# The first layer norm of a graph network: its normalising steps on GpSimd instead of VectorE

## What is computed

```python
def layer_norm(x, w, b):
    mu = jnp.mean(x, axis=-1, keepdims=True)
    var = jnp.var(x, axis=-1, keepdims=True)
    return (x - mu) * jax.lax.rsqrt(var + EPS) * w + b

h = gatv2(x, src, dst, W1s, b1s, W1d, b1d, attn1).reshape(N, DIM)
h = layer_norm(h + x, ln1_w, ln1_b)
out = gatv2(h, src, dst, Wos, bos, Wod, bod, attno).reshape(N, DIM)
```

## Time and profile before

| | before |
|---|---|
| median of three runs | 1425.2 us |
| lowest, highest | 1421.56, 1425.47 us |
| profiled execution | 1419.24 us |
| its span | 1417.4 us |
| VectorE busy | 943.6 us, 67% |
| GpSimd busy | 611.8 us, 43% |
| ScalarE busy | 564.3 us, 40% |
| TensorE busy | 1029.6 us, 73% |
| mean granted TensorE clock | 0.854 |

### The profile page before, as it was taken

The page is one execution under the profiler, slowest core; times in us unless marked ns, Lnnn a source line. Parts: engine busy times, 40 slices in busy tenths (PEclk is TensorE's granted clock), DMA queues, the critical chain, the costliest instruction groups (busy, mean ns, idle before and its releaser), DMA issues.

```text
span 1417.4 us, 15860 instructions
## 1 busy us (share of the span) xinstructions
PE 1029.6 (73%) x5499; PEld 859.4 (61%) x5499; DVE 943.6 (67%) x1678; ACT 564.3 (40%) x735; POOL 611.8 (43%) x581
## 2 busy tenths in 40 slices
PE   5956455556551677798999999618267998999982
PEld 5954333333330676797778787507245997888871
DVE  6539777777774787543544354475488655999993
ACT  3304333333331788310443434410033323777770
POOL 0026777777773000003777777787400000333330
PEclk9987877866676788899999999858687799999995
DMA  9855666666666641146777766858412126999986
GB/s 337 343 182 167 198 197 196 200 195 198 195 201 162 169 101 60 46 125 218 233 228 222 219 193 192 257 167 243 124 67 66 56 101 238 394 403 406 404 328 178
DMA packets 85033, 290.85 MB, mean 205 GB/s; under 512 B 15970, under 2 KB 37768, under 8 KB 84341
## 3 DMA queue, kind: packets, MB, share of 16 engines
q0 software_dynamic: 34656, 145.11, 33.7%
q1 hardware_dynamic: 46822, 130.71, 27.3%
q10 hardware_dynamic: 3488, 14.16, 2.5%
HBM read 258.31 MB, written 31.62 MB: 205 GB/s over the span
## 4 chain that ended last, share of the span: by engine, by line
POOL 33%; PE 29%; issue 12%; DVE 11%; DMA 9%; ACT 5%; SPq 1%; DVEq 0%; POOLq 0%; ACTq 0%
POOL dense_logits L582 12%; POOL ring_s L571 11%; POOL ring_d L577 9%; PE ps L1435 9%; PE ps L1436 9%; PE ps L1437 9%; DMA ring_d<-table_dst,dst_i 4%; ACT de L723 2%; DVE ring_s L997 1%; DVE stats L887 1%; DMA y_in<-y_rows 1%; DMA dl_b<-dense_logits 1%; DMA dl_a<-dense_logits 1%; PE ps L1526 1%; DVE tree L1098 1%
## 5 line engine op out<-in xcount | busy, mean ns | idle before, releaser
L997 DVE TENSOR_TENSOR ring_s<-ring_s,ring_d 128x776 f32<-128x776 f32 (+1 forms) x168 | 162.0, 964 | 256.9 <-DMA ring_d<-table_dst,dst_i 256.9
L571 POOL DMA_INDIRECT ring_s<-table_src,src_i x168 | 171.2, 1019 | 364.1 <-DVE fd_stage L926 301.6
L1491 PE MATMUL ps<-hot_s,hot_d 128*125 128x512 f16 (+1 forms) x840 | 181.4, 381 | 163.0 <-DVE hot_s L1004 162.8
L1491 PEld LDWEIGHTS ps<-hot_s,hot_d 128*125 128x125 f16 x840 | 114.2, 176 | 230.4 <-DVE hot_s L1004 173.2
L582 POOL DMA_INDIRECT dense_logits<-logits,cell_i x168 | 206.2, 1227 | 51.4 <-issue 50.9
L577 POOL DMA_INDIRECT ring_d<-table_dst,dst_i x168 | 163.9, 976 | 51.2 <-issue 51.2
L697 ACT ACTIVATE hot_d<-iota_h,dst_bias 128x626 f16<-128x626 f16 x84 | 68.6, 816 | 221.7 <-PE ps L1491 221.6
L1435 PE MATMUL ps<-wp,at 128*125 128x384 f32 x300 | 105.5, 352 | 10.9 <-DVE at L910 4.1
L609 POOL COPY gather_i<-lst 128x1 int32 (+1 forms) x16 | 7.4, 462 | 244.0 <-DVE lst L1355 149.0
L1436 PE MATMUL ps<-wp,at 128*125 128x384 f32 x300 | 104.1, 347 | 0.0
L1437 PE MATMUL ps<-wp,at 128*125 128x384 f32 x300 | 103.7, 346 | 0.0
(11 more groups left out here) (248 smaller groups left out, 2333.7 us busy)
## 6 DMA issues: line engine op xcount, KB each, us to landing
eraw<-in_moe_w_dram SPq DMA_DIRECT2D x50, 768.0 KB, 6.6
raw<-in_moe_w_dram SPq DMA_DIRECT2D x44, 768.0 KB, 7.3
dense_logits<-neg ACTq DMA_DIRECT2D x1, 12288.0 KB, 41.1
mix_w<-in_qkv_wT_dram SPq DMA_DIRECT2D x18, 384.0 KB, 6.3
dl_a<-dense_logits SPq DMA_DIRECT2D x2, 2187.5 KB
dl_b<-dense_logits SPq DMA_DIRECT2D x2, 2187.5 KB
y_in<-y_rows SPq DMA_DIRECT2D x5, 672.0 KB
ring_s<-table_src,src_i POOLq DMA_INDIRECT x168, 4.2
```

The costliest lines, as they stand in the source:

```text
L571: pool.indirect_dma_start(out=ring_s[:, j, 0:WL[l]], out_offset=None, in_=table_src[l], in_offset=bass.IndirectOffsetOnAxis(ap=src_i[:, t: ...
L997: dve.tensor_tensor(ring_s[:, j, 0:WL[l]], ring_s[:, j, 0:WL[l]], ring_d[:, j, 0:WL[l]], ALU.add).then_inc(z_ready[l], 1)
L1491: last = pe.matmul(ps[0:P, b, o:o + s1 - s0], hot_d[:, j, c * P:(c + 1) * P], hot_s[:, j, s0:s1], start=start and (n <= 5 or n == 9), stop ...
```

## The change

For each of the five tiles VectorE keeps the reciprocal, which now counts a new semaphore `rstd_ready`. The two instructions of `normalise_rows`, (b - mean) * w and then * rstd + bias, leave its list. GpSimd takes the tile with three instructions: `tensor_scalar` for (b - mean) * rstd, `tensor_tensor` times w, `tensor_tensor` plus bias, the second and third each behind a wait for the one before (`pool_norm`). The third counts `ln_done`. The five tiles stand in GpSimd's list between `edges(0)` and `edges(1)`. The wait for the two rows of weights moves with them.

```diff
+        rstd_ready, pool_norm = sem("rstd_ready"), sem("pool_norm")
@@ GpSimd
             edges(0)
+            pool.wait_ge(rows_loaded["ln1"], 32)
+            for t in range(T):
+                v = b1[:, t, :]
+                pool.wait_ge(rstd_ready, t + 1)
+                pool.tensor_scalar(v, v, mv[:, t, 0:1], rstd[:, t:t + 1], ALU.subtract, ALU.mult).then_inc(pool_norm, 1)
+                pool.wait_ge(pool_norm, 2 * t + 1)
+                pool.tensor_tensor(v, v, rows[0:P, 0, :], ALU.mult).then_inc(pool_norm, 1)
+                pool.wait_ge(pool_norm, 2 * t + 2)
+                pool.tensor_tensor(v, v, rows[0:P, 1, :], ALU.add).then_inc(ln_done, 1)
             edges(1)
@@ VectorE, dense(0)
                     if l == 0 and rest == 0 and 1 <= c <= T:
-                        if c == 1:
-                            dve.wait_ge(rows_loaded["ln1"], 32)
-                        ln_rstd(1, c - 1)
-                        normalise_rows(c - 1, b1[:, c - 1, :]).then_inc(ln_done, 1)
+                        dve.wait_ge(ln_std, ln_count(1, c - 1))
+                        dve.reciprocal(rstd[:, c - 1:c], std[:, c - 1:c]).then_inc(rstd_ready, 1)
```

## The result

Over 20 runs each the changed kernel takes 1431.6 us (1424.8 to 1438.0), the kernel before 1422.6 us (1416.0 to 1431.3). The ratio is 1.0058, 95% interval 1.0040 to 1.0077: slower by 8.3 us, between 5.7 and 11.0 (the two medians themselves are 9.0 apart). The forecast was +5.2 us, 1430.4 us in a range of 1423.5 to 1435.5. The direction and the range held; the forecast's size lies a little under the interval. That 1431.6 lies only 1.2 us from 1430.4 is partly luck: the forecast stood on a median of three runs, 2.6 us above the median of twenty, and that made up for most of the cost that the forecast was short of.

The account below looks back on a forecast made before the run. It took the dense stage's 22.8 us tile period to be bound by alternating stretches of VectorE and ScalarE. Port holds of 2.5 + 2.5 + 0.2 = 5.2 us on 1425.2 gave 1430.4 us, range 1423.5 to 1435.5.

Parts of the forecast that it names:

- The relief is worth nothing: Dense stage: taking 10.2 us of normalising off VectorE gains 0; the rival that it counts, 1415.0 us, had chance 0.05.
- Latency costs nothing in the stage: GpSimd's three instructions, 5.0 us a tile, end before TensorE transposes tile 4 at 594.91: cost 0.
- The port holds both ways: GpSimd's reading instructions and VectorE's two-input ones exclude each other: 5.2 us, chance 0.65; rival VectorE not held, 0.20.
- GpSimd's durations: Per tile, 1.1 us for the `tensor_scalar` and 1.7 for each `tensor_tensor`, together 5.0 us, 3.0 to 6.2.
- Tiles 0 and 1: VectorE's max tree starts late behind GpSimd's instructions, 2.5 us for each of these two tiles.
- Tile 2: GpSimd's instructions move `probs(35)` on VectorE from 554.69 to 554.88, a cost of 0.2 us.
- The sum of the stage: Port holds over the five tiles add 2.5 + 2.5 + 0.2 = 5.2 us, between 1.5 and 9.0.
- Nothing is queued behind the new waits that could be late.: GpSimd has no instruction from 440 to 650 us, so its new waits delay nothing behind them.
- The shifted clock: The shifted stage meets another TensorE clock: 2 to 3 us either way on top; chance alone 0.05.

Follow-up runs that it names:

- relief_only: The kernel before, with VectorE keeping only each tile's reciprocal and nobody doing the two normalising steps; ratio 1.0003.
- one_sqrt: The kernel before, with ScalarE's square roots of tiles 0 to 3 gathered behind the last exponential and their normalising on VectorE behind it; 1407.6 us, ratio 0.9915.
- tiles_3_4: The change for tiles 3 and 4 only, the others normalised on VectorE as in the kernel before; ratio 1.0028.
- writes_only: The kernel before, plus three GpSimd memsets of 125x2304 a tile on a scratch tile; timed once, 1420.7 us against 1420.9.
- no_scalar: The changed kernel without GpSimd's `tensor_scalar`, leaving only the two `tensor_tensor` of each tile; ratio 1.0021 against the kernel before.
- tiles_0_1: The change for tiles 0 and 1 only, the others normalised on VectorE as in the kernel before; ratio 1.0084.
- scalars_only: The kernel before, VectorE unchanged, plus three GpSimd `tensor_scalar` a tile on a scratch tile; ratio 1.0059.
- port_only: The kernel before, VectorE still normalising, plus the change's three GpSimd instructions a tile on a scratch tile; ratio 1.0100.
- late: The changed kernel, with GpSimd taking tiles 0 and 1 only once the next tile's mean and variance are done; ratio 1.0030 against the kernel before.

## Why the prediction was right, and where not

- **The relief is worth nothing.** Right, and shown by `relief_only` (periods within 0.05 us, ratio 1.0003) and by `one_sqrt` from the other side.
- **Latency costs nothing in the stage.** Right. GpSimd ended tile 4 at 598.36 and TensorE transposed it at 601.53, 3.2 us later; the forecast left 4.7. SyncE's row load went out at 598.39. `tiles_3_4` left the stage as it was.
- **The port holds both ways.** Right, and the row that was missing before is now there: 4.38 us for a tree step of 2.75. The page named in the prediction (the Trainium skill, SBUF — State Buffer, § Who interferes with whom) agrees for `tensor_tensor`. It also says that a GpSimd instruction that only writes does not meet VectorE's two-input ones; `writes_only` agrees. It says the pair is held for the whole instruction, in its line on VectorE's two-port modes, and the prediction took this for two-input instructions too. The runs come close for `tensor_tensor` (1.63 of 1.8 us) and disagree for `tensor_scalar`, which held VectorE 0.5 to 0.6 us out of 2.93.
- **GpSimd's durations.** `tensor_tensor` was put at 1.7 and measures 1.80 to 1.85, good. `tensor_scalar` was put at 1.1, upper end 1.35, and measures 2.93. This is the term of the sum that was mis-sized. It was built from rows of a memset and of an affine select, neither of which has the arithmetic of a `tensor_scalar`; a bound from other operations was taken for a bound of this one.
- **Tiles 0 and 1.** Forecast 2.5 us each, measured 3.04 and 3.07. In the forecast one of the three instructions fell on `probs(16)` and a pause took it up. In fact the `tensor_scalar` filled that pause, and both `tensor_tensor` met work without one: 1.63 + 1.48. `no_scalar` shows it: without that instruction the same two cost 1.2. That 2.5 came as near as it did is partly luck: with the measured 2.93 and 1.8, and every reading instruction holding for all its time, the prediction's own steps would put the tree of tile 0 some 4.5 us late (an estimate). A duration too short and a hold too long made up for one another.
- **Tile 2.** Forecast 0.2, measured 0.89, by the same delay: the last hold reaches `probs(35)`, which takes 1.66 us instead of 0.81, right in front of the division.
- **The sum of the stage.** 5.2 forecast, 7.0 measured, inside the bounds of 1.5 to 9.0, though the bound on `tensor_scalar` that they rest on did not hold.
- **"Nothing is queued behind the new waits that could be late."** True as to waits, and incomplete as to the cost: `edges(1)`, queued behind the new instructions on GpSimd, runs some 4 us longer by the comparison of fourteen profiles. The prediction had no such term. Stage and pass together would be about 11, the upper end of the measured interval; how they add up to 8.3 within the scatter of single profiles stays open.
- **The shifted clock.** It came in single profiles, on top, as put. The stretch between the ELU halves of tiles 3 and 4 is TensorE's. It took 21.57 us before, 21.55 after, and 19.44 in `tiles_0_1` (19.43 in `scalars_only`). So the clock had no part in the difference between before and after in this stretch. The granted clock from the first transpose there on was 0.74 before and 1.00 in `tiles_0_1` (its row: stretch, length, busy us by engine, clock, DMA):

```profile
567.20:578.20 11.00, 9.02 (x56) 8.80 (x56) 5.88 (x10) 4.61 (x5) 0.00 (x0) 0.74 0.01 1
```

```profile
572.70:581.60 8.90, 6.31 (x56) 6.10 (x56) 5.90 (x10) 4.63 (x5) 0.00 (x0) 1.00 0.01 2
```

## What to carry to other kernels

Before moving work to a quieter engine, ask which engine sets the pause that the work lies in. If the work sits in another engine's stretch, taking it away is worth nothing, and that other engine's list (here two table loads a tile) is where the time is. Work moved to GpSimd is not free beside VectorE: count the reading time of its two-input instructions, and look at what VectorE has queued at the moment they come, since 3.0 us a tile became 1.2 when the two came 2.9 us earlier.

## What the runs showed of the hardware

- On GpSimd the one-input `tensor_scalar` is slower than the two-input `tensor_tensor`: 2.94 against 1.80 us for 125x768 f32, a copy 0.82, a memset 0.74. But where it holds VectorE's two-input instructions it does so for 0.5 to 0.6 us (`port_only`, `scalars_only`); in the change it ran right beside `probs(16)`, which took 0.83 us instead of 0.81. `tensor_tensor` holds for up to some 1.6.
- A memset of GpSimd holds nobody (`writes_only`), and VectorE's subtraction with one operand in PSUM kept its 0.94 us inside a GpSimd `tensor_tensor` (after).
- VectorE's `tensor_scalar` can be held although it has a single SBUF operand. In `late` one of 125x8 (0.17 us elsewhere) took 1.83 us at 555.06, beside a GpSimd `tensor_tensor` from 555.04 to 556.86, and the one of 125x768 took 0.95 instead of 0.56. At 576.54 that of 125x8 took 1.77 us, behind GpSimd's L616, which itself had waited for VectorE's L927. VectorE and then GpSimd in order of time:

```profile
574.06 2.56 DVE L927 TENSOR_TENSOR wp<-wraw,wp 128x2304 fp32r<-128x2304 f32 x1 [4.96 <-ACT wp L686]
576.54 1.77 DVE L1166 TENSOR_SCALAR rden<-den 125x8 f32<-125x8 f32 x1
```

```profile
574.12 4.16 POOL L616 TENSOR_TENSOR b<-b,rows 125x768 f32<-125x768 f32 x1
```

- Having run a `tensor_scalar` on GpSimd, even of 125x8 and 200 us earlier, goes with an indirect-DMA pass some 4 us longer (fourteen profiles). The cause stays open.
